# Two tiles' rows from early gathers, and three chunks of sines moved behind the setup block, in a fused embedding, attention and routing kernel

## The chip, the cores and the metric

The kernel runs on one core of a Trainium2 chip, as one launch. The metric is the device time of the launch in microseconds. The kernel before was timed three times: 1538.4, 1539.6 and 1539.77 us, median 1539.6 us.

## The reference

16384 tokens (128 sequences of 128) pass an embedding, one attention layer and one mixture layer. Cut to what matters here:

```python
# 1. token table: 12500 rows of 128 floats
freqs = arange(1, 129)
sin_table = sin((num_value / 1000)[:, None] * freqs[None, :])
table = where(is_num[:, None], sin_table, weight)
h = table[x]                                   # x: (128, 128) token numbers
# 2. attention with 8 heads of 64, per sequence of 128
n = (h - mean(h)) / sqrt(var(h) + eps)
q, k, v = n @ Wq, n @ Wkv
dots = where(eye, -1e-9, (q @ k.T) * scale)    # heads are mixed before ...
attn = mix_post(softmax(mix_pre(dots)))        # ... and behind the softmax
h = h + (attn @ v) @ Wout + bout
# 3. h + a shared feed-forward + two banks of 8 experts, top-1 routed, capacity 1280
```

All arithmetic is in float32. Matrix products that need the precision are built from three products of a high and a low part (`_hi`, `_lo`).

## The kernel before

Four blocks follow each other: setup, attention, experts, shared feed-forward. Each block holds one instruction list per engine (PE for matmuls, DVE for vector work, ACT for activations, POOL, and SP, which issues DMAs). The order within a list is written out by hand, and semaphores order the lists among each other. A block ends when all five lists have ended.

**Setup** builds the table in HBM. The 12500 rows are laid over 128 partitions, 97 rows each; the last 84 rows form a 98th column (`VS` = 98). Eight columns are a chunk (`VC` = 8), so there are 13 chunks (`CHUNKS`), and the last has two columns. SP loads the weight rows of each chunk into `h_sb`. The numbers of all rows are turned into thousandths by nine small DVE instructions (L553 to L561), split into halves (`num_hl`), transposed by PE, and copied to `numT` by ACT. Then chunk for chunk: PE multiplies numbers by frequencies (`angles`, into `ps_a`), ACT rounds to whole turns (`whole_turns`, L421), DVE subtracts them in two instructions (`reduce`, L584 and L585), POOL clamps (`clamp`, L340), ACT takes the sine (`sines`, L436), DVE puts the sines over the rows that are numbers (`put_sines`, L591, a predicated copy), and SP writes the chunk to the table (L401). Beside it the setup folds the attention weights into two matrices M and N: POOL and ACT make `mixed`, PE multiplies (`product`, L521), ACT and DVE split into `M_hi`, `M_lo`, `N_hi`, `N_lo`.

**Attention** handles one tile of 128 tokens at each step k, as a software pipeline over all engines that starts at k = -12 and is written as `step(i, k)` for each engine. POOL gathers the table rows of tile k+10 (L778, one indirect DMA each, into 8 buffers `got`), adds `bout` for tile k+7 (L785, five at once at k = -3), and computes deviations of four tiles at once (L806 to L808). DVE takes mean and variance of tile k+8 (L1112, L1121) and normalizes two tiles (L1039, `normalize`). PE transposes them (L874), ACT and DVE split them (L1000, L1139), PE multiplies with M into `ps_w` in four quarters q (L885 to L887), ACT and DVE split these (L992, L1081). Then come scores (L857), the predicated copy of the scores (L1066), the maximum (L1072), exponentials (L961), sums and products with N, the residual, and the router. In front of the pipeline PE runs `WARM` = 24 matmuls of the identity (L951).

Of the kernel before, what the change touches and what calls it, by code (L numbers as in the profile page):

```python
# [16 lines left out]
F32 = mybir.dt.float32  # L17
# [40 lines left out]
WARM = 24  # L58
# [10 lines left out]
VC = 8  # L69
CHUNKS = -(-VS // VC)  # L70

# [119 lines left out]

class RouterConstants:


    def __init__(self, sb):
# [8 lines left out]
        self.mv2 = [sb(f"mv2_{k}", [P, 4, 2]) for k in range(2)]  # L204
        self.token_i, self.token = sb("token_i", [P, TILES], I32), sb("token", [P, TILES])
# [32 lines left out]
def setup(nc, x, weight, num_value, is_num, Wq, Wkv, scale, mix_pre, mix_post, Wout,  # L238
# [6 lines left out]
    def rows_of(c):  # L245
        return VC if c < CHUNKS - 1 else VS - VC * (CHUNKS - 1)

    def cols(c):
        return slice(c * CH, c * CH + rows_of(c) * D)

    with ExitStack() as s:
# [10 lines left out]
        num_i = sb("num_i", [P, VS], I32)  # L262
        num_f = sb("num_f", [P, VS])
        part = sb("part", [P, 4, VS])
# [4 lines left out]
        mask = sb("mask", [P, VS], I32)  # L269
# [22 lines left out]
        names = ("made", "num", "num_f", "numT", "numT_out", "angle", "whole", "reduced", "clamped", "sine", "done", "put",  # L292
# [8 lines left out]
        LAST_COL = slice(VR * D, VS * D)  # L301

# [4 lines left out]
        def _(pool):  # L307
# [27 lines left out]
            made["head_of"] = link.n  # L335

            def clamp(c):
                a = angle[c % 3][:, 0:rows_of(c) * D]
                pool.wait_ge(S["reduced"], c + 1)
                nc.gpsimd.tensor_scalar(a, a, PI_BELOW, -PI_BELOW, ALU.min, ALU.max).then_inc(S["clamped"], 1)  # L340
# [6 lines left out]
            for c in range(CHUNKS):  # L347
# [20 lines left out]
                if c == 2:  # L368
                    link.wait()
                    link.inc(nc.gpsimd.tensor_copy(C.token[:, :], C.token_i[:, :]))  # L370
                    link.inc(nc.gpsimd.memset(zeros[:, :, D], float(DROPPED)))
            link.wait()

        @block.sync
        def _(sp):
            sp.dma_start(num_i[:, 0:VR], num_value[0:P * VR].rearrange("(p r) -> p r", p=P)).then_inc(S["num"], 16)
            sp.dma_start(isn[:, 0:VR], is_num[0:P * VR].rearrange("(p r) -> p r", p=P)).then_inc(S["num"], 16)
            sp.wait_ge(S["made"], made["pads"])
            sp.dma_start(num_i[0:REST, VR:VS], num_value[P * VR:VOCAB].rearrange("(p o) -> p o", o=1)).then_inc(S["num"], 16)
            sp.dma_start(rest_isn[0:REST, 0:1], is_num[P * VR:VOCAB].rearrange("(p o) -> p o", o=1)).then_inc(S["num"], 16)  # L380
# [6 lines left out]
            for c in range(1, CHUNKS - 1):  # L387
                need(sp, s_row[c % 4], 16 * (c // 4))
                sp.dma_start(h_sb[:, cols(c)], w_main[:, cols(c)]).then_inc(s_row[c % 4], 16)
            one = slice((CHUNKS - 1) * CH, VR * D)  # L390
            sp.wait_ge(s_row[(CHUNKS - 1) % 4], 16 * ((CHUNKS - 1) // 4))
            sp.dma_start(h_sb[:, one], w_main[:, one]).then_inc(s_row[(CHUNKS - 1) % 4], 16)
            sp.dma_start(h_sb[0:REST, LAST_COL], weight[P * VR:VOCAB, :]).then_inc(s_row[(CHUNKS - 1) % 4], 16)
# [5 lines left out]
            for c in range(CHUNKS - 1):  # L399
                sp.wait_ge(S["done"], c + 1)  # L400
                sp.dma_start(t_main[:, cols(c)], h_sb[:, cols(c)]).then_inc(S["put"], 16)  # L401
            sp.wait_ge(S["done"], CHUNKS)
            sp.dma_start(t_main[:, one], h_sb[:, one]).then_inc(S["put"], 16)
            sp.dma_start(table[P * VR:VOCAB, :], h_sb[0:REST, LAST_COL]).then_inc(S["put"], 16)
            sp.wait_ge(S["put"], 16 * (5 + CHUNKS + 1))

        @block.scalar
        def _(act):
# [3 lines left out]
            def rest_of_numbers():  # L412
                act.wait_ge(S["numT"], 2)
                nc.scalar.activation(numT[:, 4 * P:12 * P], ps_m[0:KR, :], ACT.Copy).then_inc(S["numT_out"], 1)
                nc.scalar.activation(numT[:, 12 * P:13 * P], ps_c[0:KR, 0:P], ACT.Copy).then_inc(S["numT_out"], 1)

            def whole_turns(c):
                w = rows_of(c) * D
# [14 lines left out]
            def sines(c):  # L433
                a = angle[c % 3][:, 0:rows_of(c) * D]
# [3 lines left out]
            for c in range(CHUNKS + 2):  # L438
# [18 lines left out]
                if c in (5, 6, 8):  # L457
                    remix({5: 1, 6: 2, 8: 3}[c])
                if c in (7, 9):
                    prefill((c - 7) // 2)  # L460
# [1175 lines left out]
```

## Time and profile before

| what | value |
| --- | --- |
| median of three runs | 1539.6 us |
| profiled execution | 1540.3 us |
| its span in the trace | 1538.6 us |
| busy: PE, ACT, DVE, POOL | 96%, 75%, 68%, 63% of the span |
| mean DMA rate | 82 GB/s |

Around the span lie 1.7 us that the trace doesn't show. The span can be cut by engine lists: setup until 67.7 us, where the first instructions of the attention block start, then the attention block. The slices of the page show PE at six to seven tenths busy in the first two slices of 38.5 us, nine tenths and more in nearly all that follow. The two first slices hold setup and the filling of the attention pipeline.

A row of the timeline says when a group of instructions started, how long they were busy together, the engine, the line, what is written from what, and in brackets how long the engine had been idle and what released it.

### The profile page before, as it was taken

The numbers are of one execution on the slowest core, as the hardware profiler recorded it, in microseconds if no ns is written. First come the engines' busy times: TensorE is split into PE (matmuls) and PEld (weight loads), VectorE is DVE, ScalarE is ACT, GpSimd is POOL, SyncE is SP. The second block draws the span as 40 slices with busy tenths as digits, with TensorE's granted clock in tenths as the row PEclk, the third lists the DMA queues.
The fourth block names the chain that finished last, engine by engine and source line by source line (L and its number), as shares of the span: only waits on it lengthen the run. The fifth ranks groups of instructions, "written<-read, shape, count | busy, mean of one in ns | idle before, by whom it ended". The sixth has DMA issues, their size and how long they took to land. (4 is left out here: it accounts for less than half of the span.)

```text
span 1538.6 us, 33795 instructions
## 1 busy us (share of the span) xinstructions
PE 1482.0 (96%) x11149; PEld 1371.7 (89%) x11149; DVE 1049.3 (68%) x2801; ACT 1146.6 (75%) x3461; POOL 971.1 (63%) x992
## 2 busy tenths in 40 slices
PE   6679999999999999999999999988999999999999
PEld 3368999999999999999999999978999999999999
DVE  7777787787877887787877887764334343346665
ACT  5468888888888888888888888874555555545555
POOL 6665558788788878878878887664577656510000
PEclk9889999999999999999999999999999999999999
DMA  6322321121121111111111111012344224456665
GB/s 254 137 105 105 115 66 52 52 67 40 40 59 38 39 57 35 35 49 42 34 35 54 35 35 51 25 39 62 80 114 114 72 69 109 119 152 186 184 182 149
DMA packets 170603, 126.35 MB, mean 82 GB/s; under 512 B 29539, under 2 KB 154061, under 8 KB 170432
## 3 DMA queue, kind: packets, MB, share of 16 engines
q1 hardware_dynamic: 153024, 104.05, 22.7%
q0 software_dynamic: 17408, 20.16, 4.8%
q8 instruction: 91, 1.49, 0.4%
q14 instruction: 80, 0.66, 0.2%
HBM read 61.63 MB, written 78.56 MB: 91 GB/s over the span
## 5 line engine op out<-in xcount | busy, mean ns | idle before, releaser
L961 ACT ACTIVATE expd<-masked,nmax 128x128 f32<-128x128 f32 x1024 | 395.7, 393 | 0.0
L763 POOL TENSOR_TENSOR prob<-expd,rtotal 128x1024 f32<-128x1024 f32 x128 | 243.0, 1898 | 143.4 <-DVE rtotal L1049 142.5
L1066 DVE COPY_PREDICATED masked<-off_diag,ps_s 128x1024 f32<-128x1024 int32 x128 | 175.2, 1369 | 146.9 <-PE ps_s L857 146.9
L899 PE MATMUL ps_o<-u,probT 128*128 128x128 f32 x2048 | 249.2, 275 | 2.9 <-issue 2.9
L899 PEld LDWEIGHTS ps_o<-u,probT 128*128 128x128 f32 x2048 | 239.1, 192 | 3.1 <-issue 3.1
L961 ACT ACTIVATION_READ_ACCUMULATOR expd<-masked,nmax 128x1 f32 x1024 | 196.5, 192 | 0.0
L970 ACT ACTIVATE u<-ps_ut 128x1024 f32<-128x1024 f32 x128 | 131.4, 1026 | 64.0 <-PE ps_ut L910 64.0
L1081 DVE TENSOR_TENSOR w_lo<-ps_w,w_hi 128x512 fp32r<-128x512 f32 x256 | 164.3, 680 | 4.3 <-ACT w_hi L992 4.3
L985 ACT ACTIVATE probT<-ps_ut 128x1024 f32<-128x1024 f32 x128 | 131.4, 1027 | 45.0 <-PE ps_ut L865 38.5
L992 ACT ACTIVATE w_hi<-ps_w 128x512 fp32r<-128x512 f32 x256 | 146.3, 596 | 18.6 <-PE ps_w L887 12.1
L885 PE MATMUL ps_w<-xT_hi,M_hi 128*128 128x256 f32 x512 | 155.2, 303 | 2.7 <-DVE xT_lo L1139 2.7
L1072 DVE TENSOR_REDUCE nmax<-masked 128x8 f32<-128x1024 f32 x128 | 155.5, 1215 | 2.5
L619 POOL DMA_INDIRECT sent_fq<-x,to_row x128 | 125.7, 982 | 42.0 <-issue 38.4
L619 POOL DMA_INDIRECT sent_sp<-x,to_row x128 | 130.9, 1022 | 31.3 <-issue 24.1
L778 POOL DMA_INDIRECT got<-table,gi x128 | 130.6, 1020 | 24.9 <-issue 12.6
L886 PE MATMUL ps_w<-xT_hi,M_lo 128*128 128x256 f32 x512 | 144.3, 282 | 0.0
L887 PE MATMUL ps_w<-xT_lo,M_hi 128*128 128x256 f32 x512 | 144.3, 282 | 0.0
L1564 ACT ACTIVATE sh_hid<-sh_ps_h,b 128x256 f32<-128x256 f32 x224 | 87.7, 475 | 75.4 <-PE sh_ps_h L1536 75.4
L865 PEld LDWEIGHTS ps_ut<-ident,prob 128*128 128x128 f32 x1024 | 115.3, 140 | 25.3 <-issue 15.5
L865 PE MATMUL ps_ut<-ident,prob 128*128 128x128 f32 x1024 | 133.6, 273 | 3.3 <-ACT u L970 3.3
L1427 POOL DMA_INDIRECT answers_fq<-res,tokens x80 | 81.1, 1014 | 54.5 <-DVE res L1406 37.5
L1545 PE MATMUL sh_ps_o<-w,sh_hid 128*128 128x128 f32 x896 | 109.1, 275 | 0.1
(231 smaller groups left out, 3881.4 us busy)
## 6 DMA issues: line engine op xcount, KB each, us to landing
turned<-x2T SPq DMA_DIRECT2D x32, 256.0 KB, 2.2
answers_sp<-zeros SPq DMA_DIRECT2D x16, 512.0 KB, 5.0
answers_fq<-zeros SPq DMA_DIRECT2D x16, 512.0 KB, 4.1
xT<-turned SPq DMA_DIRECT2D x56, 128.0 KB, 2.5
sh_back<-answers_sp SPq DMA_DIRECT2D x56, 128.0 KB, 2.3
sh_back<-answers_fq SPq DMA_DIRECT2D x56, 128.0 KB, 2.5
out<-res SPq DMA_DIRECT2D x56, 128.0 KB, 2.0
h_sb<-in_L_tok_weight SPq DMA_DIRECT2D x12, 512.0 KB, 5.7
```

The lines of the kernel that those rows point to most:

```text
L619: nc.gpsimd.indirect_dma_start(sent[b], bass.IndirectOffsetOnAxis(ap=to_row[(t // BATCH) % 2][:, c:c + 1], axis=0), x2[:, t % 16, :], None ...
L763: nc.gpsimd.tensor_tensor(prob[k % 2][:, :].rearrange("p (g j) -> p g j", g=H), expd[k % 2][:, :].rearrange("p (g j) -> p g j", g=H), rtot ...
L865: mm = nc.tensor.transpose(ps_ut[:, g * N:(g + 1) * N], prob[(k - 3) % 2][:, g * N:(g + 1) * N], ident[:, :])
L885: nc.tensor.matmul(o, M_hi, xT_hi[:, m % 4, :], start=True, stop=False)
L886: nc.tensor.matmul(o, M_lo, xT_hi[:, m % 4, :], start=False, stop=False)
L887: mm = nc.tensor.matmul(o, M_hi, xT_lo[:, m % 4, :], start=False, stop=True)
L899: mm = nc.tensor.matmul(ps_o[:, 0:D], probT[k % 2][:, g * N:(g + 1) * N], u[k % 2][:, g * D:(g + 1) * D], start=(g == 0), stop=(g == H - 1))
L961: ins = nc.scalar.activation(expd[(k - 1) % 2][:, g * N:(g + 1) * N], masked[(k - 1) % 2][:, g * N:(g + 1) * N], ACT.Exp, bias=nmax[(k - 1 ...
L992: nc.scalar.activation(w_hi[m % 2][:, :, 2 * q:2 * q + 2, :].rearrange("p b g j -> p g b j"), ps_w[q % 2][:, :].rearrange("p (g b j) -> p ...
L1066: nc.vector.copy_predicated(masked[k % 2][:, :].rearrange("p (g j) -> p g j", g=H), off_diag[:, :].unsqueeze(1).to_broadcast([P, H, N]), p ...
L1072: nc.vector.tensor_reduce(nmax[k % 2][:, :], masked[k % 2][:, :].rearrange("p (g j) -> p g j", g=H), X_AXIS, ALU.max, negate=True).then_in ...
L1081: nc.vector.tensor_tensor(dst, ps_w[q % 2][:, :].rearrange("p (g b j) -> p g b j", g=2, b=2), hi.bitcast(F32), ALU.subtract).then_inc(S["w ...
```

## The change

- SP loads the token numbers of the first two tiles (`ids0`) early. POOL gathers by them the numbers (`num_i`), the flags (`isn0`) and the weight rows of both tiles: six indirect DMAs in front of its first clamp. They become columns 99 and 100 of the layout in `h_sb` (`VX` = 100), so that the last chunk now has four columns. It is worked on as eighth of the thirteen (`ORDER`).
- The thousandths, the halves and the transpose of these columns are separate instructions (DVE after the second `reduce`, PE and ACT at the sixth chunk). Means and deviations of the two tiles are computed in the setup, and attention normalizes them from `h_sb`.
- The last three chunks in the new order (`LATES` = 3) are reduced and clamped in the setup, in unused columns of `h_sb`. Two of their sines run in the setup, the third first in attention's ACT list. Their predicated copies and their table writes stand at the start of the attention block, and POOL waits for these three writes (`s_late`) before its first gather, which is that of tile 2.
- DVE's list at the start of attention is written out anew: tile 0 and 1, late copies, four quarters of `w_lo`, then the statistics of tiles 2 and 3; those of tiles 4 to 7 and the normalization of tiles 2 and 3 stand inside step 0.
- `M_lo` moves behind the last `reduce`, and the identity matmuls (now 18) into the setup's PE list.

The diff, cut to its core:

```diff
-WARM = 24
+WARM = 18
+VX = VS + 2
+ORDER = (*range(7), CHUNKS - 1, *range(7, CHUNKS - 1))
+LATES = 3
+ON_TIME = CHUNKS - LATES
...
@@ setup, gpsimd
+            pool.wait_ge(S["ids0"], 16)
+            for t in range(2):
+                nc.gpsimd.indirect_dma_start(num_i[:, VS + t:VS + t + 1], None, num_value...).then_inc(S["num0"], 16)
+            for t in range(2):
+                nc.gpsimd.indirect_dma_start(isn0[:, t:t + 1], None, is_num...).then_inc(S["rows0"], 16)
+                nc.gpsimd.indirect_dma_start(h_sb[:, (VS + t) * D:(VS + t + 1) * D], None, weight, ...).then_inc(S["rows0"], 16)
...
+                if c == 10:
+                    link.wait()
+                    pool.wait_ge(S["stat0"], 1)
+                    link(nc.gpsimd.tensor_scalar(C.var[:, 0:2], C.mv1[0][:, 0:2, 1], 1.0, EPS, ALU.mult, ALU.add))
+                    link.inc(nc.gpsimd.tensor_tensor(C.rstd0[:, :], C.var[:, 0:2], C.power[:, 0:2], ALU.pow))
+            pool.wait_ge(S["clamped"], CHUNKS)
...
@@ setup, tensor
+                if c == 5:
+                    pe.wait_ge(S["num_f"], 2)
+                    pe.wait_ge(S["wT_out"], 3)
+                    number_rows(CHUNKS - 1).then_inc(S["numT"], 1)
                 if 5 <= c:
                     for half in range(2):
                         product((c - 5) // HC, (c - 5) % HC, half)
+            pe.wait_ge(S["reduced"], CHUNKS - 1)
+            for _ in range(WARM):
+                nc.tensor.matmul(ps_a[CHUNKS % 2][:, 0:P], ident[:, :], ident[:, :], start=True, stop=True)
...
@@ setup, vector
-            dve.wait_ge(S["num"], 64)
+            dve.wait_ge(S["num"], 32)
...
             for c in range(CHUNKS):
                 reduce(c)
-                if c >= 2:
+                if c == 1:
+                    dve.wait_ge(S["num0"], 32)
+                    thousandths(slice(VS, VX))
+                    halves(slice(CHUNKS - 1, CHUNKS), VX - VC * (CHUNKS - 1))
+                if 0 <= c - 2 < ON_TIME:
                     put_sines(c - 2)
...
-                if c == 11:
-                    dve.wait_ge(S["hi"], 1)
-                    link.inc(... mats["M_lo"] ...)
-            put_sines(CHUNKS - 2)
-            put_sines(CHUNKS - 1)
+                if c == 9:
+                    dve.wait_ge(S["done"], 8)
+                    for t in range(2):
+                        link.inc(nc.vector.bn_stats(C.stat0[:, t, :], h_sb[:, (VS + t) * D:(VS + t + 1) * D]))
+                    link.wait()
+                    for t in range(2):
+                        ins = nc.vector.bn_aggr(C.mv1[0][:, t, :], C.stat0[:, t, :])
+                    ins.then_inc(S["stat0"], 1)
+            dve.wait_ge(S["hi"], 1)
+            link.inc(... mats["M_lo"] ...)
...
@@ attention, sync
+            for n, c in enumerate(ORDER[ON_TIME:]):
+                sp.wait_ge(S["late_done"], n + 1)
+                sp.dma_start(t_main[:, chunk_cols(c)], h_sb[:, chunk_cols(c)]).then_inc(s_late, 16)
             load_expert(sp, bank, 0, first, first.loaded)
...
@@ attention, gpsimd
+                if k == -8:
+                    pool.wait_ge(s_late, 16 * LATES)
...
+                if k == -3:
+                    deviations(i, 0)
                 for t in range(5) if k == -3 else (k + 7,) if k > -3 and live(i, k + 7) else ():
...
@@ attention, vector
+                if k == 0:
+                    dve.wait_ge(S["first_rstd"], 1)
+                    normalize(2)
+                    low_x(1)
+                    first_stats(4, 4, S["stat1"])
...
+            normalize(0)
+            late_rows(0)
+            low_x(0)
+            late_rows(1)
+            dve.wait_ge(S["late_sine"], 1)
+            late_rows(2)
+            for q in range(4):
+                low_w(0, q)
+            first_stats(2, 2, S["first_stat"])
             pipelined(dve, step, BODY, FIRST, LAST, LEAD, END, link, VCHAIN)
```

How the instructions stand at three places, in the order of each engine's list.

DVE in the setup, from the second instruction of the second `reduce` on, before:

```order
L585 SCALAR_TENSOR_TENSOR angle<-turns,ps_a 128x1024
L584 SCALAR_TENSOR_TENSOR ps_a<-turns,ps_a 128x1024
L585 SCALAR_TENSOR_TENSOR angle<-turns,ps_a 128x1024
L591 COPY_PREDICATED h_sb<-mask,angle 128x1024
L584 SCALAR_TENSOR_TENSOR ps_a<-turns,ps_a 128x1024
```

and now, from the same instruction on (the third `reduce` follows behind these rows):

```order
L655 SCALAR_TENSOR_TENSOR angle<-turns,ps_a 128x1024
L621 CAST part<-num_i 128x2
L622 TENSOR_SCALAR part<-part 128x2
L623 TENSOR_SCALAR part<-part 128x2
L624 TENSOR_TENSOR part<-part 128x2
L625 TENSOR_TENSOR part<-part 128x2
L626 TENSOR_TENSOR part<-part 128x2
L627 SCALAR_TENSOR_TENSOR part<-part 128x2
L628 SCALAR_TENSOR_TENSOR part<-part 128x2
L629 SCALAR_TENSOR_TENSOR num_f<-part 128x2
L634 CAST num_hl<-num_f 128x4
L635 TENSOR_TENSOR num_hl<-num_f,num_hl 128x4
```

Eleven instructions on two columns have come between the second and the third `reduce`.

POOL at the start of attention, before. The rows start at the gathers of tiles 0 to 3 and end with that of tile 8:

```order
L778 DMA got<-table,gi 128x128 x4
L775 COPY gi<-ids 128x4
L778 DMA got<-table,gi 128x128
L792 TENSOR_SCALAR var<-mv_0 128x2
L793 TENSOR_TENSOR rstd<-var,power 128x2
L778 DMA got<-table,gi 128x128
L792 TENSOR_SCALAR var<-mv_0 128x2
L793 TENSOR_TENSOR rstd<-var,power 128x2
L778 DMA got<-table,gi 128x128 x2
L785 TENSOR_TENSOR h_sb<-got,bout_b 128x128 x5
L775 COPY gi<-ids 128x4
L778 DMA got<-table,gi 128x128
```

and now, from behind the gathers of tiles 2 and 3 to the gather of tile 8:

```order
L883 COPY gi<-ids 128x4
L887 DMA got<-table,gi 128x128 x2
L903 TENSOR_SCALAR var<-mv_0 128x2
L904 TENSOR_TENSOR rstd<-var,power 128x2
L887 DMA got<-table,gi 128x128 x2
L859 TENSOR_SCALAR var<-mv_1 128x4
L860 TENSOR_SCALAR var<-mv_0 128x4
L861 TENSOR_TENSOR rstd<-var,power 128x8
L896 TENSOR_TENSOR h_sb<-h_sb,bout_b 128x128 x2
L896 TENSOR_TENSOR h_sb<-got,bout_b 128x128 x3
L883 COPY gi<-ids 128x4
L887 DMA got<-table,gi 128x128
```

The deviations of tiles 4 to 7 (L859 to L861) have moved from behind the gather of tile 10 to in front of the gather of tile 8.

DVE in step 0 of attention, from the predicated copy of tile 0's scores to that of tile 1, before:

```order
L1066 COPY_PREDICATED masked<-off_diag,ps_s 128x1024
L1072 TENSOR_REDUCE nmax<-masked 128x8
L1081 TENSOR_TENSOR w_lo<-ps_w,w_hi 128x2x2x128 x2
L1039 TENSOR_SCALAR x_0<-got,mv_1,rstd 128x128 x2
L1112 BN_STATS stat<-got 128x6
L1121 BN_AGGR mv_0<-stat 128x2
L1066 COPY_PREDICATED masked<-off_diag,ps_s 128x1024
```

and now, from tile 3's statistics (in front of step 0) on. Behind this piece, three more pairs L1163 and L1165 follow, then the two `w_lo`, tiles 4 and 5 normalized, tile 8's statistics, and the copy for tile 1:

```order
L1163 BN_STATS stat<-got 128x6
L1165 BN_AGGR mv_0<-stat 128x2
L1194 COPY_PREDICATED masked<-off_diag,ps_s 128x1024
L1200 TENSOR_REDUCE nmax<-masked 128x8
L1140 TENSOR_SCALAR x_1<-got,mv_0,rstd 128x128 x2
L1147 TENSOR_TENSOR xT_lo<-ps_x,xT_hi 128x256
L1163 BN_STATS stat<-got 128x6
L1165 BN_AGGR mv_1<-stat 128x2
```

Between the first copy of scores and the second now stand ten instructions more: the normalization and the low part of tiles 2 and 3, and the statistics of tiles 4 to 7.

## Rows read from the trace of the kernel before

**Rows 1.** Windows: busy time of each engine in a stretch, clock, DMA share, GB/s.
```profile
116.00:1130.00 1014.00, 1002.48 (x7330) 919.08 (x7329) 763.42 (x2040) 849.59 (x2709) 751.46 (x752) 1.00 0.18 53
```
**Rows 2.** Waits of DVE, 13 to 66 us: total, times, longest.
```profile
DVE ps_a L584 <- ACT turns L421: 6.1, 4, 3.4
```
**Rows 3.** Timeline of the setup, DVE's chunk loop: start, busy, engine, line.
```profile
14.10 1.23 DVE L584 SCALAR_TENSOR_TENSOR ps_a<-turns,ps_a 128x1024 f32<-128x1024 int32 x1 [3.43 <-ACT turns L421]
...
51.20 1.30 DVE L591 COPY_PREDICATED h_sb<-mask,angle 128x1024 f32<-128x1024 int32 x1
52.40 1.23 DVE L584 SCALAR_TENSOR_TENSOR ps_a<-turns,ps_a 128x1024 f32<-128x1024 int32 x1
...
64.98 0.67 DVE L612 TENSOR_TENSOR N_lo<-ps_c,N_hi 128x512 fp32r<-128x512 f32 x1
```
**Rows 4.** Groups by line and shape, DVE, 4 to 13 us.
```profile
L554 DVE TENSOR_SCALAR part<-part 128x98 f32<-128x98 f32 x1 | 1.1, 1059 | 0.0
L553 DVE CAST part<-num_i 128x98 f32<-128x98 int32 x1 | 0.5, 457 | 4.5 <-DMA rest_isn<-in_L_tok_is_num 4.5
L566 DVE CAST num_hl<-num_f 128x2 fp32r<-128x2 f32 x1 | 0.2, 160 | 0.0
```
**Rows 5.** Timeline of the setup around the sixth and seventh chunk.
```profile
30.55 3.75 PE L521 MATMUL ps_m<-mixed,wkT 128*128 128x512 f32 x4 [0.79 <-POOL mixed L343]
30.72 0.59 ACT L454 ACTIVATE wvT<-ps_t 128x512 f32<-128x512 f32 x1
...
36.54 1.23 DVE L584 SCALAR_TENSOR_TENSOR ps_a<-turns,ps_a 128x1024 f32<-128x1024 int32 x1 [1.09 <-ACT turns L421]
```
**Rows 6.** Timeline around the end of the setup.
```profile
65.05 0.80 SPq L404 DMA_DIRECT2D table<-h_sb  x1
67.69 0.33 SPq L228 DMA_DIRECT2D w<-in_L_ffn_W_sp  x1
```
**Rows 7.** Waits of SP's queue, 60 to 68 us.
```profile
SPq L251 <- DMA table<-h_sb: 1.3, 1, 1.3
```
**Rows 8.** Timeline of SP from 59.7 us: three table writes, the first at 59.71.
```profile
59.71 4.79 SPq L401 DMA_DIRECT2D table<-h_sb  x3
```
**Rows 9.** Window of one microsecond behind that write.
```profile
62.00:63.00 1.00, 0.00 (x0) 0.00 (x0) 1.00 (x2) 0.00 (x0) 1.00 (x1) 0.50 0.00 0
```
**Rows 10.** DMA issues, 58 to 90 us: count, median us to landing.
```profile
got<-table,gi POOLq DMA_INDIRECT x11, 2.6
```
**Rows 11.** Timeline of POOL at the start of attention.
```profile
68.50 1.19 POOL L778 DMA_INDIRECT got<-table,gi  x1 [0.60 <-POOL gi L775]
...
71.27 0.95 POOL L778 DMA_INDIRECT got<-table,gi  x1 [0.30 <-issue]
...
80.94 2.11 POOL L785 TENSOR_TENSOR h_sb<-got,bout_b 128x128 f32<-128x128 f32 x5
...
83.45 0.99 POOL L778 DMA_INDIRECT got<-table,gi  x1 [0.27 <-POOL gi L775]
...
88.79 1.68 POOL L808 TENSOR_TENSOR rstd<-var,power 128x8 f32<-128x8 f32 x1
```
**Rows 12.** Timeline of DVE in attention's first steps.
```profile
72.40 0.29 DVE L1112 BATCH_NORM_STATS2 stat<-got 128x6 f32<-128x128 f32 x1 [6.74 <-DMA got<-table,gi]
...
88.32 1.37 DVE L1066 COPY_PREDICATED masked<-off_diag,ps_s 128x1024 f32<-128x1024 int32 x1 [1.02 <-PE ps_s L857]
...
92.99 1.33 DVE L1066 COPY_PREDICATED masked<-off_diag,ps_s 128x1024 f32<-128x1024 int32 x1
...
98.92 1.34 DVE L1066 COPY_PREDICATED masked<-off_diag,ps_s 128x1024 f32<-128x1024 int32 x1 [1.32 <-PE ps_s L857]
```
**Rows 13.** Timeline of PE: scores of tile 2 and of tile 4.
```profile
96.92 0.70 PE L857 MATMUL ps_s<-w_hi,xT_hi 128*128 128x512 f32 x2 [2.40 <-DVE w_lo L1081]
...
108.07 0.70 PE L857 MATMUL ps_s<-w_hi,xT_hi 128*128 128x512 f32 x2 [0.30 <-DVE w_lo L1081]
```
**Rows 14.** Window of two microseconds at tile 2's scores.
```profile
98.00:100.00 2.00, 2.00 (x10) 1.81 (x9) 1.08 (x1) 0.49 (x4) 1.73 (x3) 0.50 0.19 74
```

More of the change, by code:

```diff
@@ L301, in setup, with angle_of @@
         LAST_COL = slice(VR * D, VS * D)
+        loaded = {}
+        for i, c in enumerate(ORDER):
+            loaded[i] = loaded.get(i - 4, 0) + (32 if c == CHUNKS - 1 else 16)
+        def angle_of(i):
+            return angle[i % 3][:, 0:rows_of(ORDER[i]) * D] if i < ON_TIME else late_angles(h_sb, i - ON_TIME)
         made = {}
@@ L398, in _ @@
                 sp.dma_start(dst, src).then_inc(S["put"], 16)
[L399 to L405, printed above, removed]
+            for i, c in enumerate(ORDER[:ON_TIME]):
+                sp.wait_ge(S["done"], i + 1)
+                if c < CHUNKS - 1:
+                    sp.dma_start(t_main[:, cols(c)], h_sb[:, cols(c)]).then_inc(S["put"], 16)
+                else:
+                    sp.dma_start(t_main[:, one], h_sb[:, one]).then_inc(S["put"], 16)
+                    sp.dma_start(table[P * VR:VOCAB, :], h_sb[0:REST, LAST_COL]).then_inc(S["put"], 16)
+            for k in range(4):
+                sp.wait_ge(s_row[k], max(n for i, n in loaded.items() if i % 4 == k))
+            sp.wait_ge(S["put"], 16 * (5 + ON_TIME + 1))
         @block.scalar
@@ L530, in _ @@
             angles(1)
-            for c in range(4, CHUNKS):
+            for c in range(4, CHUNKS - 1):
                 ins = number_rows(c)
@@ L567, in _, with thousandths @@
-            link.wait()
-            for part_of, whole in ((slice(0, CHUNKS - 1), slice(0, VC)), (slice(CHUNKS - 1, CHUNKS), slice(0, last))):
-                n = VC if part_of.start == 0 else last
-                src = num_f[:, part_of.start * VC:part_of.start * VC + (part_of.stop - part_of.start) * n].rearrange("p (c r) -> p c r", r=n)
-                nc.vector.tensor_tensor(num_hl[:, part_of, whole, 1], src, num_hl[:, part_of, whole, 0].bitcast(F32),
-                                        ALU.subtract).then_inc(S["num_f"], 1)
+            def thousandths(at):
+                value, q, hi, lo = (part[:, n, at] for n in range(4))
+                link(nc.vector.tensor_copy(value, num_i[:, at]))
+                link(nc.vector.tensor_scalar(q, value, 0.001, None, ALU.mult))
+                link(nc.vector.tensor_scalar(hi, q, 4097.0, None, ALU.mult))
+                link(nc.vector.tensor_tensor(lo, hi, q, ALU.subtract))
+                link(nc.vector.tensor_tensor(hi, hi, lo, ALU.subtract))
+                link(nc.vector.tensor_tensor(lo, q, hi, ALU.subtract))
+                link(nc.vector.scalar_tensor_tensor(hi, hi, -1000.0, value, ALU.mult, ALU.add))
+                link(nc.vector.scalar_tensor_tensor(lo, lo, -1000.0, hi, ALU.mult, ALU.add))
+                link(nc.vector.scalar_tensor_tensor(num_f[:, at], lo, 0.001, q, ALU.mult, ALU.add))
@@ L689, in attention @@
         s_got = [sem(f"a_got{k}") for k in range(8)]
+        s_late = sem("a_late_put")
         s_sent = [sem(f"a_sent{k}") for k in range(8)]
@@ L948, in step @@
                         mm.then_inc(S["head_down"], 1)
-            for _ in range(WARM):
-                nc.tensor.matmul(ps_o[:, 0:D], ident[:, :], ident[:, :], start=True, stop=True)
             pipelined(pe, step, BODY, FIRST, LAST, LEAD, END)
```

243 lines of the change are left out of this document (141 added, 102 removed).

## The prediction

> **What bounds the kernel now.** I read the windows first. Behind 116 us PE is busy for 1002.5 of 1014 us at the full granted clock [rows 1], and nothing of the change touches what runs there. So the change counts only by how much earlier or later the attention pipeline reaches the state in which PE never waits. The scores of tile 4 are the marker for that: they start at 108.07 after a short wait for DVE [rows 13], and PE has nearly no gap behind them. The second view is the timeline from 0 to 108 us, followed backwards from there: tile 4's scores wait for `w_lo` from DVE, whose list from 88.32 on runs nearly without idle time [rows 12]. In front of it lies the chain table write, gather, statistics, deviation, normalize. The setup ends by a table write that SP waits 1.3 us for [rows 7]. DVE bounds the setup's chunk loop: all its waits there sum to 6.1 us, 3.4 of them ahead of the first `reduce` [rows 2, 3].
>
> **The setup, as DVE's sum.** Before, DVE runs from 14.10 to 65.65 [rows 3]. The terms, in us:
> - Start. DVE was released by the fourth of four small loads [rows 4] and now waits for the first two. SP issues them about 0.45 apart: -0.9.
> - Three full predicated copies leave. In the dense part one costs 52.40 - 51.20 = 1.2 [rows 3]: -3.6.
> - Eleven small instructions come behind the second `reduce`. Such a one is busy 0.16 [rows 4], 0.21 with the gap to the next dependent one: 2.3. From below 1.8. From above 4.5, because a like instruction took 1.06 [rows 4] while POOL worked, and here POOL clamps the second chunk meanwhile. I take 2.8, near the lower row, as only the first three have that form: +2.8.
> - The last chunk has four columns and not two: `reduce` +0.5, copy +0.3 (the 1024-wide 1.2 scaled by width): +0.8.
> - Flag copy, two statistics, two aggregations: 0.2 + 2 x 0.33 + 2 x 0.2: +1.3.
> - Waits. Before, beside the first, they are 6.1 - 3.4 = 2.7. The one ahead of the third `reduce` (1.4) is filled by the small instructions. The one ahead of the seventh (1.1) [rows 5] grows: PE now waits until ACT has copied `wvT`, done at 31.31, and transposes (0.4), while the products began at 30.55 [rows 5]. That puts the products, and the next chunk's angles behind them in PE's list, 1.2 later. Together about -0.4.
>
> The sum is 0.0: DVE ends at about 65.65 again. What the copies free, the added work takes. But the block then ends by DVE and no longer by the write: before, the wait ended at 65.85 + 1.3 = 67.15 and the next block began at 67.69 [rows 6, 7], so the change of blocks costs 0.55. Now it begins at 66.2: **-1.5**. POOL's last clamp ends about half a microsecond before DVE. The six gathers cost POOL 1.25 each [rows 11] in a stretch in which its list was empty, from about 8.5 until the first `reduce` ends at 14.10 + 2 x 1.23 = 16.6 [rows 3]: 7.5 in 8.1, hidden, with no room to spare. The identity matmuls now lie beside the last `reduce`. That costs nothing.
>
> The Trainium skill, page "GPSIMD Engine Reference", in the table of the engine's properties, has GpSimd share its SBUF interfaces with VectorE, with contention where a VectorE instruction uses both ports. By it the first three small instructions could each wait for the clamp, and the small ones would cost 4.5, not 2.8. The 1.06 row [rows 4] agrees with it, but does not show it alone.
>
> **Attention, counted from the start T of its block.** Before, T = 67.69. Tile 8's gather starts at T+15.8 [rows 11] and the copy of tile 1's scores at T+25.3 [rows 12].
>
> Now DVE first normalizes (0.65), makes three late copies (3 x 1.2) and a low part (0.4): T+4.65. Only then can the third late write be issued. A write of this size issued at 59.71 had left the queues by 62.0 [rows 8, 9]; with completion I take 2.5 (bounds 2.3 and 3.4). POOL's first gather starts at T+7.15 and the second 1.25 later, landing 2.6 behind its start [rows 10]: T+11.0. The upper bound for a landing is 72.40 - 68.50 = 3.9 [rows 11, 12]. Tile 0's scores are ready at about T+10.3 (by the early rows this is 9 us sooner than before), but DVE's statistics of tiles 2 and 3 stand ahead of their copy, so that begins at T+11.6.
>
> Then DVE's list: copy 1.35 [rows 12], maximum 1.2 (the same width), normalize 0.6, the round over PE and ACT for the low part 1.4, four pairs of statistics 2.4 (an estimate, 0.6 a pair): T+18.6. POOL waits for these: deviations 1.7 [rows 11] and two small instructions ahead, 2.25 together; five additions 2.1 [rows 11]; index copy with its gap 0.5; and only then tile 8's gather, at T+23.5 where it was T+15.8. It lands 2.6 later. DVE's statistics of tile 8 stand in front of the copy of tile 1's scores: T+26.7 with the pair's 0.55. Against T+25.3 that is **+1.4**. So the nine microseconds won on tile 0's scores are all given back at the gather of tile 8.
>
> From there the list is as before. Before, the next copy is 5.93 later and waits 1.32 for tile 2's scores [rows 12], which took 2.0 because the clock went to 0.50 in their last third (granted 0.50 from 98 to 100 [rows 14]). With six equal passes, four at 2.4 and two at 1.2 GHz, all six cost 1.5 at 2.4 GHz and 3.0 at 1.2 GHz. PE now idles some 7 us ahead of these scores where it was 2.4 [rows 13], so I expect them at 1.2 GHz for the most part: between -0.5 and +1.0, **+0.9** taken. ACT is further ahead: **-0.3**, a small wait of DVE for it at tile 3.
>
> **Sum.** -1.5 + 1.4 + 0.9 - 0.3 = +0.5. The profiled execution took 1540.3 us (span 1538.6 and 1.7 around it) and would take 1540.8. It lies 0.7 above the median of the runs, so the forecast is 1540.1 us. About 3.1 us (0.2%) is what a measurement of this kernel can tell from no change.
>
> The terms' bounds: setup from 2.5 earlier to 2.5 later than my value (small instructions 1.8 to 4.5, the wait at the seventh chunk 0 to 2.3), write and gathers from -0.5 to +2.2, clock from -1.4 to +0.1. The likeliest case alone covers 1537 to 1543.
>
> **Rivals.**
> 1. *The gather of tile 8 is not what DVE waits for* (faster). If POOL is through sooner, or the gathers land sooner, the copy of tile 1's scores follows tiles 4 and 5's normalization: deviations end at T+20.9, normalize 0.6 and a pair 0.55, so T+22.1, 4.6 less. That gives 1535.5, and 1534.8 with tile 2's scores half at the full clock. For it: the whole early part is ready nine microseconds sooner. Against it: the order of POOL's list, which is fixed, and 1.25 a gather. Chance 0.24.
> 2. *PE's clock* (slower). PE has only scattered work from T+10 to T+31. If it stays at 1.2 GHz not for tile 2's scores only but until tile 4's, two more scores (+1.5 each by the estimate above) come onto the path, which gives 1543.1, and more if it falls again later. It decides from the point at which PE, and not DVE, ends last at tiles 3 and 4. For it: 0.50 at 98 us after a gap of only 2.4 us. Against it: DVE has 5 us of work per tile, which covers a slow PE in part. Chance 0.14. The Trainium skill, page "TensorE: Matmul & The Clock Gate", section "HAM oscillation — how this bites in real kernels", tells of kernels whose PE falls to half rate in every wait and starts each piece cold. By that rule this rival is the case, and the trace agrees at 98 us.
> 3. *The rebuilt setup is longer* (no measurable change, or slower). Six gathers hold the first clamp, the small instructions cost 4.5, PE's wait at the sixth chunk passes on in full: DVE ends 2.5 later, 1542.6. For it: none of these has room to spare. Chance 0.12.
>
> The forecast keeps 0.50. Faster by more than 0.2%: nearly all of rival 1 and 0.02 of the forecast's own spread, 0.25. Slower: 0.11 of rival 2, 0.05 of rival 3, 0.04 of the forecast, 0.20. The rest is 0.55. Range 1535.0 to 1543.4.
>
> **What would show it.** Right: DVE's last instruction of the setup within a microsecond of 65.6 and the attention block from about 66.2; eleven small instructions in 2 to 3.5 us; POOL's first gather 7 us into the block and that of tile 8 near T+23.5, with DVE's longest wait named after it; tile 4's scores within 1.5 us of 108.1. Wrong: no wait of DVE for that gather, a block start outside 64 to 68.5, PE at half pace for tiles 3 and 4, or any difference behind 116 us, where I expect none.

## The result: 0.14% slower, and the profile after

The changed kernel takes 1540.05 us (median of 20 runs, 1537.91 to 1543.35), the kernel before 1538.04 us in as many runs beside it (1536.56 to 1540.22). The ratio is 1.0014, interval [1.0007, 1.0020]: 2.0 us slower, inside the 0.2% that the prediction counted as no change, and 0.05 us from its 1540.1. That close a hit is luck, since two errors cancel. The forecast was a change of +0.5, and the two profiled spans differ by 2.2 (1538.6 and 1540.8): 1.7 more. But it was added to 1539.6, the median of the first three runs of before, and twenty runs have 1538.04: 1.6 less.

Where the 2.2 us arise is seen in three places. First the setup, in the timeline of DVE after (start, busy, engine, line, operation, in brackets the idle time before it and what ended it):

```profile
13.38 1.23 DVE L654 SCALAR_TENSOR_TENSOR ps_a<-turns,ps_a 128x1024 f32<-128x1024 int32 x1 [1.08 <-ACT turns L480]
...
18.18 0.16 DVE L621 CAST part<-num_i 128x2 f32<-128x2 int32 x1
18.37 1.04 DVE L622 TENSOR_SCALAR part<-part 128x2 f32<-128x2 f32 x1
19.44 0.31 DVE L623 TENSOR_SCALAR part<-part 128x2 f32<-128x2 f32 x1
19.79 0.16 DVE L624 TENSOR_TENSOR part<-part 128x2 f32<-128x2 f32 x1
...
21.25 1.22 DVE L654 SCALAR_TENSOR_TENSOR ps_a<-turns,ps_a 128x1024 f32<-128x1024 int32 x1
...
38.46 1.23 DVE L654 SCALAR_TENSOR_TENSOR ps_a<-turns,ps_a 128x1024 f32<-128x1024 int32 x1 [2.16 <-ACT turns L480]
...
52.14 1.60 DVE L212 COPY_PREDICATED h_sb<-is_number,angle 128x512 f32<-128x512 int32 x1
...
65.75 0.68 DVE L692 TENSOR_TENSOR N_lo<-ps_c,N_hi 128x512 fp32r<-128x512 f32 x1
67.04 0.60 DVE L1140 TENSOR_SCALAR x<-h_sb,mv,first_rstd 128x128 f32<-128x128 f32 x2 [0.61 <-PEq L278]
```

The first `reduce` is 0.72 sooner than in [rows 3], the eleven small instructions take 3.1 us (18.18 to 21.25), one of them 1.04 for two columns, the copy of the four-column chunk takes 1.60, and the seventh `reduce` is 1.9 later than in [rows 5] behind a wait of 2.16 instead of 1.09. DVE ends at 66.43. The block starts at T = 67.02 instead of 67.69, 0.67 sooner.

Second POOL, from the block's start on, the rows that answer to [rows 11]:

```profile
67.02 0.18 POOL L883 COPY gi<-ids 128x4 int32<-128x4 int32 x1 [1.79 <-POOLq L278]
75.48 1.10 POOL L887 DMA_INDIRECT got<-table,gi  x1 [8.28 <-DMA table<-h_sb]
...
86.77 0.19 POOL L859 TENSOR_SCALAR var<-mv 128x4 f32<-128x4 f32 x1 [2.68 <-DVE mv L1165]
87.04 0.19 POOL L860 TENSOR_SCALAR var<-mv 128x4 f32<-128x4 f32 x1
87.32 1.66 POOL L861 TENSOR_TENSOR rstd<-var,power 128x8 f32<-128x8 f32 x1
88.97 0.87 POOL L896 TENSOR_TENSOR h_sb<-h_sb,bout_b 128x128 f32<-128x128 f32 x2
89.80 1.29 POOL L896 TENSOR_TENSOR h_sb<-got,bout_b 128x128 f32<-128x128 f32 x3
91.05 0.18 POOL L883 COPY gi<-ids 128x4 int32<-128x4 int32 x1
91.51 1.08 POOL L887 DMA_INDIRECT got<-table,gi  x1 [0.28 <-POOL gi L883]
```

The first gather waits 8.28 us for the third late write, and tile 8's, the last row, has deviations and additions ahead of it: T+24.5 where it was T+15.8. What DVE makes of that (answering to [rows 12]):

```profile
71.53 0.69 DVE L1153 TENSOR_TENSOR w_lo<-ps_w,w_hi 128x512 fp32r<-128x512 f32 x1
...
78.34 0.29 DVE L1163 BATCH_NORM_STATS2 stat<-got 128x6 f32<-128x128 f32 x1 [2.45 <-DMA got<-table,gi]
...
79.98 1.26 DVE L1194 COPY_PREDICATED masked<-off_diag,ps_s 128x1024 f32<-128x1024 int32 x1
...
94.17 0.29 DVE L1241 BATCH_NORM_STATS2 stat<-got 128x6 f32<-128x128 f32 x1 [4.25 <-DMA got<-table,gi]
94.50 0.18 DVE L1250 BATCH_NORM_AGGREGATE mv<-stat 128x2 f32<-128x6 f32 x1
94.60 1.27 DVE L1194 COPY_PREDICATED masked<-off_diag,ps_s 128x1024 f32<-128x1024 int32 x1
...
101.41 1.34 DVE L1194 COPY_PREDICATED masked<-off_diag,ps_s 128x1024 f32<-128x1024 int32 x1 [2.25 <-PE ps_s L956]
```

Tile 0's copy begins at 79.98, tile 1's only at 94.60, behind a wait of 4.25 us for tile 8's gather. That is T+27.6, where before it was T+25.3. Third the clock, in PE's timeline (answering to [rows 13]) and in windows (busy time of each engine, then the granted clock, DMA share, GB/s; answering to [rows 14] and [rows 1]):

```profile
98.47 1.19 PE L956 MATMUL ps_s<-w_hi,xT_hi 128*128 128x512 f32 x2 [6.69 <-DVE w_lo L1153]
99.46 1.05 PE L956 MATMUL ps_s<-w_lo,xT_hi 128*128 128x512 f32 x2
100.31 1.05 PE L956 MATMUL ps_s<-w_hi,xT_lo 128*128 128x512 f32 x2
...
110.27 0.70 PE L956 MATMUL ps_s<-w_hi,xT_hi 128*128 128x512 f32 x2 [0.32 <-DVE w_lo L1153]
```

```profile
116.00:1130.00 1014.00, 1002.26 (x7315) 918.30 (x7315) 763.40 (x2039) 849.42 (x2713) 751.84 (x751) 1.00 0.18 52
...
98.00:100.00 2.00, 1.53 (x4) 1.27 (x5) 1.13 (x5) 0.43 (x3) 0.76 (x1) 0.50 0.15 41
100.00:102.00 2.00, 2.00 (x8) 1.71 (x7) 0.59 (x1) 0.00 (x0) 1.73 (x3) 0.50 0.00 0
```

PE has idled 6.69 us and makes all of tile 2's scores at the half clock (granted 0.50, 1.2 GHz), so tile 2's copy stands 6.81 behind tile 1's instead of 5.93: +0.88. Tile 4's scores come 8.86 behind that copy instead of 9.15: -0.29. The sum is -0.67 + 2.28 + 0.88 - 0.29 = 2.2, the marker's own shift (110.27 against 108.07) and the whole difference of the spans. Behind 116 us PE is as busy as before.

### The profile page after: what moved, and what is told of

Read it like the earlier page. It is cut to its first block and busy times, and to the rows that moved or that the text cites. A ratio compares the mean times of both kernels' runs of the same rounds, so it can differ in the third digit from the quotient of the medians.

```text
span 1540.8 us, 33791 instructions
## 1 busy us (share of the span) xinstructions
PE 1483.2 (96%) x11137; PEld 1370.2 (89%) x11137; DVE 1055.4 (68%) x2811; ACT 1147.2 (74%) x3461; POOL 974.1 (63%) x996
## 5 line engine op out<-in xcount | busy, mean ns | idle before, releaser
L699 POOL DMA_INDIRECT sent_sp<-x,to_row x128 | 131.0, 1024 | 32.8 <-issue 24.5
```

The costliest lines, as they stand in the source:

```text
L699: nc.gpsimd.indirect_dma_start(sent[b], bass.IndirectOffsetOnAxis(ap=to_row[(t // BATCH) % 2][:, c:c + 1], axis=0), x2[:, t % 16, :], None ...
```

## The experiments

Twelve runs, each timed twelve times, on three chips: e1 to e4 on one, c0 and e5 to e7 on the second, e8 to e11 on the third. The kernel before, beside them, takes 1570.6 to 1573.0 us there. The traces of such runs show more idle time on PE behind 800 us, not in the part studied here. Each ratio is against the kernel before on the same chip, with an interval some 0.3% wide, so the trace has to decide most questions. All times below are of this table: T is the start of POOL's first instruction in the block; "copy 1" is the start of tile 1's copy; "2 - 1" what tile 2's copy comes behind it; "scores 4" the start of tile 4's scores.

| run | 7th reduce (its wait) | T | first gather | copy 1 | 2 - 1 | scores 4 | ratio, interval |
|---|---|---|---|---|---|---|---|
| c0_after | 37.52 (1.21) | 66.29 | T+8.48 | 93.57 | 6.82 | 109.55 | 1.0026 [1.0010, 1.0041] |
| e1_gather8_first | 37.75 (1.46) | 66.32 | T+8.55 | 89.74 | 6.86 | 105.27 | 0.9981 [0.9965, 0.9996] |
| e2_loads_behind_writes | 37.94 (1.65) | 66.53 | T+8.14 | 94.67 | 6.81 | 110.64 | 1.0036 [1.0017, 1.0054] |
| e3_filler | 37.52 (1.22) | 66.76 | T+8.45 | 96.23 | 6.94 | 111.84 | 1.0019 [1.0004, 1.0033] |
| e4_transpose_later | 37.40 (1.09) | 65.96 | T+8.46 | 93.56 | 6.80 | 109.11 | 1.0011 [0.9994, 1.0028] |
| e5_no_small_ones | 35.57 (0.98) | 64.36 | T+8.44 | 91.70 | 6.81 | 107.69 | 1.0025 [1.0009, 1.0041] |
| e6_gather8_and_transpose | 36.86 (0.57) | 65.44 | T+8.57 | 88.86 | 6.73 | 104.25 | 0.9992 [0.9975, 1.0008] |
| e7_filler26 | 38.45 (2.16) | 67.03 | T+8.40 | 95.79 | 5.56 | 110.03 | 1.0015 [0.9995, 1.0035] |
| e8_best_and_filler16 | 37.25 (0.95) | 65.83 | T+8.54 | 89.23 | 6.52 | 104.42 | 0.9982 [0.9967, 0.9998] |
| e9_two_late | 38.44 (2.16) | 68.53 | T+7.25 | 94.78 | 6.81 | 110.25 | 1.0006 [0.9991, 1.0020] |
| e10_two_late_and_best | 37.38 (1.08) | 67.47 | T+7.28 | 89.61 | 6.46 | 104.76 | 0.9963 [0.9943, 0.9982] |
| e11_warm24 | 38.45 (2.17) | 67.13 | T+8.50 | 95.82 | 6.81 | 111.80 | 1.0020 [1.0009, 1.0032] |

**The changed kernel again.** Its edit is none.

> The changed kernel itself, once more, beside the kernels below on one chip. First measurement: 1.0014 [1.0007, 1.0020] times before. Expected: the same within 0.1%, tile 4's scores about 43 us after the attention block's first instruction (110.27 - 67.02 there).

The ratio is 1.0026, 0.12% above the first 1.0014, with an interval that holds it. T+43.3 for tile 4's scores, as expected. The seventh `reduce`, though, comes at 37.52 and not at 38.46, with nothing changed. The timeline of PE of this run shows why:

```profile
32.49 3.28 PE L584 MATMUL ps_m<-mixed,wkT 128*128 128x512 f32 x4
35.70 0.72 PE L549 MATMUL ps_a<-freq,numT 16*128 16x512 f32 x2
```

and that of the changed kernel's first trace:

```profile
32.47 3.75 PE L584 MATMUL ps_m<-mixed,wkT 128*128 128x512 f32 x4
36.15 1.22 PE L549 MATMUL ps_a<-freq,numT 16*128 16x512 f32 x2
```

The same products start at the same time. Two passes of the angles behind them take 0.72 us in one execution and 1.22 in the other, where PE's passes get this short only from 41 us on. The windows give a granted clock of 1.00 for both stretches, so here the durations have to tell the clock: two passes of this width take 0.70 at tile 4's scores, at the full clock, and 1.19 at tile 2's, at the half clock. That is worth 0.9 us at this `reduce` and varies between executions, so single traces of the setup are compared below only where these products have the same duration.

**Tile 8's and 9's gathers first.**

```diff
 # POOL, step k == -3
+fetch(-2)          # gathers of tiles 8 and 9, taken out of the next two steps,
                    # without their wait for `resid`
+fetch(-1)
 deviations(i, 0)
 # then the five additions
```

> The changed kernel, but POOL issues the gathers of tiles 8 and 9 right behind that of tile 7, ahead of the deviations of tiles 4 to 7 and the five additions (their buffers are free, since tiles 0 and 1 no longer use them). Theory A (DVE's wait for the gather of tile 8, 4.25 us, gives back what the early tiles win): that wait is gone, the copy of tile 1's scores starts at about T+23.7 instead of T+27.6 (T the start of the attention block), the scores of tile 4 start some 3.8 us earlier, near 106.5, and the time falls by 3 to 4 us against the changed kernel, 1 to 2 us below the kernel before. Rival B (PE's clock sets the pace of the first steps): the wait goes, but the scores of tile 4 move by less than 1.5 us. Rival C (the rebuilt setup is the loss): no more than 1 us.

POOL's and DVE's timelines of this run:

```profile
83.94 0.97 POOL L889 DMA_INDIRECT got<-table,gi  x1 [0.27 <-POOL gi L884]
85.22 0.95 POOL L889 DMA_INDIRECT got<-table,gi  x1 [0.31 <-issue]
```

```profile
89.32 0.28 DVE L1247 BATCH_NORM_STATS2 stat<-got 128x6 f32<-128x128 f32 x1
89.74 1.33 DVE L1200 COPY_PREDICATED masked<-off_diag,ps_s 128x1024 f32<-128x1024 int32 x1
```

The wait of 4.25 us in front of tile 8's statistics is gone, tile 1's copy stands at T+23.4 instead of T+27.3 (c0), tile 4's scores 4.3 sooner than in c0 (5.0 sooner than in the first trace, where 3.8 was expected; 0.7 of it lies in the start of the block), and the kernel is faster than before. The gather of tile 8, held by POOL's own list, is what cost the time: theory A.

**The weight loads behind the late writes.**

```diff
+sp.wait_ge(s_late, 16 * LATES)
 load_expert(sp, bank, 0, first, first.loaded)
```

> The changed kernel, but SP waits for the three late table writes before it issues the first expert's weight loads. Theory A (the third write lands 3.9 us behind its issue because it shares the queues with the other late writes and with these loads): POOL's first gather starts 1.0 to 1.3 us earlier in the block (T+7.3 and not T+8.5), and so does everything up to the scores of tile 4; the time falls by about 1 us. Rival (a write of this size takes that long by itself, or the pile-up is among the three writes): the first gather moves by less than 0.4 us and the time stays.

The first gather comes at T+8.14, 0.34 sooner than in c0: so little of the late landing is due to the loads. The loads now run beside the gather instead, and its reader waits longer: the statistics of tile 2 start 4.3 behind its gather's start, 3.1 in c0 (one execution each). The rival is right, and nothing is gained.

**Identity products ahead of tile 2's scores, 40 and 26.**

```diff
 # PE, behind step 1's liftings (range(26) in e7)
+for _ in range(40):
+    nc.tensor.matmul(ps_o[:, 0:D], ident[:, :], ident[:, :], start=True, stop=True)
```

> The changed kernel, and 40 identity matmuls on PE in step 1, in the 6.7 us in which PE now waits for tile 2's w_lo. Theory A (the idle time in front of tile 2's scores lets the clock fall, and these six passes at 1.2 GHz cost 2.9 us instead of 1.5): the granted clock stays at 1.00 from 92 to 102 us, tile 2's scores end 0.9 to 1.4 us earlier, and DVE's wait for them falls from 2.25 to about 1; the time falls by about 1 us. Rival (DVE's work hides the slow clock): the scores of tile 4 move by less than 0.3 us.

> The changed kernel with 26 instead of 40 identity products of 128 columns on PE ahead of tile 2's scores; 40 had run past the point where the scores could start (101.49 instead of near 100.1). Theory A (the half clock costs 0.9 us in tile 2's scores and has no later effect): scores at full clock, tile 2's copy 5.9 to 6.1 us behind tile 1's (6.81 in the changed kernel), tile 4's scores 0.8 us sooner; time 0.05% under, which the timing hardly shows. Rival B (the clock is at full speed again through tile 2's own scores anyway; the filler only moves where it rises): copy 6.8 behind, nothing gained.

The timelines of PE, first of the 40 and then of the 26:

```profile
92.64 9.09 PE L991 MATMUL ps_o<-ident 128*128 128x128 f32 x80
101.49 0.71 PE L956 MATMUL ps_s<-w_hi,xT_hi 128*128 128x512 f32 x2
```

```profile
99.69 0.70 PE L956 MATMUL ps_s<-w_hi,xT_hi 128*128 128x512 f32 x2 [1.89 <-DVE w_lo L1156]
100.23 0.62 PE L956 MATMUL ps_s<-w_lo,xT_hi 128*128 128x512 f32 x2
100.69 0.62 PE L956 MATMUL ps_s<-w_hi,xT_lo 128*128 128x512 f32 x2
```

I had priced an identity product at 0.1 us. It is two passes and takes 0.22, so 40 of them took 8.9 us (92.64 to 101.49) and held up the scores that they were to speed up: the expectation for e3 failed by that. With 26 the scores run at full clock and tile 2's copy is 5.56 behind tile 1's instead of 6.81. From tile 1's copy to tile 4's scores it is 14.24 instead of 15.98 (c0) or 15.67 (the first trace). So the half clock costs 1.25 there, the gain holds up to tile 4, and a clock that falls in a wait is a real cost here: what the Trainium skill tells on the page "TensorE: Matmul & The Clock Gate", section "HAM oscillation — how this bites in real kernels", holds in this place, for 1.25 us and for one tile's scores. Against c0 the marker did not improve all the same, since DVE waits longer for tile 8's gather: 5.24 us here and 4.91 in e3, where the seven runs without filler and with that gather in its old place have 4.20 to 4.27. The wait grows behind the gather's start: from it to the statistics pass 3.7 us in e7 and 3.3 in e3, 2.7 in the first trace. The DMA view of e7 from 93 to 94 us, while the gather is under way, has one transfer of another queue, which it calls `q8 instruction`; e3 has one in the same microsecond; in the seven others it comes behind 96 us, when the gather has landed. That the products on PE pull this transfer forward, onto the gather, fits both runs, but is not shown.

**The last chunk's transpose a chunk later.**

```diff
-if c == 5:        # PE, and ACT's copy likewise
+if c == 6:
     pe.wait_ge(S["num_f"], 2)
```

> The changed kernel, but the transpose of the last chunk's numbers, with its wait for ACT's copy of wvT, stands one chunk later in PE's list (behind the angles of the seventh chunk), and ACT's copy of it ahead of that chunk's remix. Theory A (this wait delays PE's products and the angles behind them, so that DVE waits 2.2 us and not 1.1 for the seventh reduce, and the delay runs through to the end of the setup): DVE's wait falls to about 1.1, DVE's last setup instruction and the scores of tile 4 come about 1 us earlier, the time falls by about 1 us. Rival (the next wait takes its place, as the eighth chunk's angles now need the transposed numbers soon after): less than 0.3 us.

The products of the mixing matrices start at 31.40 instead of 32.49, and the seventh `reduce` waits 1.09 instead of 2.16. Against the first trace, whose products also ran at the half clock, the block starts 1.06 sooner and tile 4's scores are 1.16 sooner. The pair e9 and e10 shows it a second time at like clock (38.44 and 37.38). Theory A; the timing alone could not tell it.

**The eleven small instructions left out.**

```diff
+halves(slice(CHUNKS - 1, CHUNKS), 2)     # ahead, with the first splitting
 # DVE, behind the second reduce
-dve.wait_ge(S["num0"], 32)
-thousandths(slice(VS, VX))
-halves(slice(CHUNKS - 1, CHUNKS), VX - VC * (CHUNKS - 1))
```

> The changed kernel without the eleven instructions that make the pairs of the two gathered columns (3.1 us between the second and the third reduce on DVE, 18.18 to 21.33); the thousandths of the gathered numbers are left out of the computation, and a small cast pair stands in the first splitting. Theory A (they stand on the path of the sines): the third reduce starts near 18.3 instead of 21.3, and the attention block's start moves from 67.0 to 64.2 (by up to 3 us, less 0.2 for the larger splitting); tile 1's copy and tile 4's scores move along by as much: time 0.18% under the changed kernel's. Rival B (the setup is bound by PE's products of the mixing matrices or by the sine engine, which fill the gap): the block starts less than 1 us sooner.

```profile
19.31 1.23 DVE L655 SCALAR_TENSOR_TENSOR ps_a<-turns,ps_a 128x1024 f32<-128x1024 int32 x1 [1.05 <-ACT turns L480]
```

This kernel leaves the thousandths of the first two tiles' numbers out of the computation. The third `reduce` starts 1.96 sooner than in c0 and not 3, because it now waits 1.05 for ACT: a third of the small work had lain in a wait. T and tile 4's scores both move by 1.9. The setup passes this on in full: theory A, smaller by the wait. The ratio (1.0025) does not show the 1.9 us.

**Both gains together, and with 16 identity products.** e6 is e1 and e4 in one; e8 adds the loop of e7 with 16.

> Both edits that brought something in the first four together: tile 8's and 9's gathers right behind tile 7's, and the last chunk's transpose a chunk later. If they add (theory A: one acts on the setup's end, the other on the gathers behind it), tile 4's scores start 5.0 + 1.1 = 6.1 us before the changed kernel's 110.27, near 104.2, less 0.7 that the first may have had by chance; time 0.34% under the changed kernel's, ratio to before about 0.998. Rival: the later start of the gathers' wait (the third write) eats the transposes' share, since the write's landing is bound by the amount of data: then only 5.0.

> The version with tile 8's and 9's gathers behind tile 7's and the late transpose, and 16 identity products on PE in the gap ahead of tile 2's scores (2.42 us of PE's idle time there, which 16 products of 0.1 us at the half clock fill but for 0.7). Theory A (what PE did ahead sets the clock of tile 2's scores, as 26 of them did in the changed kernel, where tile 2's copy came 5.56 us behind tile 1's instead of 6.81): tile 2's copy 5.6 to 6.0 us behind tile 1's (6.73 without them), tile 4's scores 0.7 to 1.0 us sooner, near 103.4; ratio to before near 0.998. Rival B (16 are too few: the clock stays at its half through these scores): 6.7 behind and nothing gained, or up to 0.3 lost.

In e6 tile 4's scores are at 104.25, 5.3 before c0's and 6.0 before the first trace's (expected 6.1). They add. In e8 the 16 products take 3.7 us (twice what I had priced), so that the scores start at 94.08 at full clock, with no gap ahead: the copies are 6.52 apart instead of 6.73. They start 4.9 behind tile 1's copy, 0.9 more than in e6 (3.9), which eats the clock's gain. As e10 has 6.46 without any filler, even the 0.2 are not shown. Neither theory was tested as meant, since 16 were too many and not too few.

**Two late chunks, alone and with both gains.**

```diff
-LATES = 3
+LATES = 2          # and one `late_rows` less in DVE's list at the start of attention
```

e10 has the edits of e6 besides.

> The changed kernel with two chunks' sines taken beside attention's first turns instead of three. Theory A (the first gather waits for the last late write, which waits for three writes' data, 1.5 MB at 300 to 400 GB/s): the third write's share, 1.3 us of DVE and up to 1.4 us of pile-up, moves ahead of the block; one copy (1.3 us) goes back into the setup, so the block starts 1.2 to 1.4 us later, and the first gather comes 6.0 to 6.9 us behind it instead of 8.48: tile 4's scores from 0.4 later to 0.8 sooner than 109.55. Rival B (the last write lands as long after its issue with two as with three): first gather 7.2 behind, tile 4's scores at the same time within 0.2.

> Two late chunks, with tile 8's and 9's gathers behind tile 7's and the late transpose. If the effects add: 104.25 plus what two late chunks alone bring or cost against 109.55 (-0.8 to +0.4), ratio to before 0.998 to 0.9995. Rival: with the gathers no longer in the way, DVE's own work is the bound up to tile 1's copy, and the copy moved into the setup costs its 1.3 us in full: near 105.5.

e9 against the first trace (seventh `reduce` at 38.44 and 38.46): T is 1.5 later, the first gather 1.2 nearer to T, tile 1's copy 0.2 later, tile 4's scores at 110.25 and 110.27. Rival B: the last write lands as long after its issue with two as with three, and one copy more or less in the block is an even exchange. The view of the late writes' line (`--source L811`) gives their times from issue to landing, the longest being the last write's:

```profile
DMA to landing us min/median/max: 2.6/2.6/3.1
```

for the changed kernel,

```profile
DMA to landing us min/median/max: 2.6/2.8/3.0
```

for e9, and for e2, without the loads beside them:

```profile
DMA to landing us min/median/max: 2.6/2.6/2.7
```

e10 has tile 4's scores at 104.76, 0.1 above the upper end of what was expected (103.45 to 104.65) and below the rival's 105.5, and the lowest ratio of all, 0.9963 [0.9943, 0.9982]: a version that beats both kernels, the one before by 0.2 to 0.6%. That it beats e1, e6 or e8 is not shown; their intervals overlap, and its marker is no earlier than theirs.

**24 products at the setup's end instead of 18.**

```diff
-WARM = 18
+WARM = 24
```

> The changed kernel with 24 identity products at the end of the setup, as before, instead of 18. Theory A (PE waits for the first lifting of the block anyway, and the clock falls in the wait for the gathers whatever stands ahead of it): nothing: tile 1's copy 27.3 us behind the block's start, tile 4's scores 43.3 behind, ratio as the changed kernel's (1.0014 to 1.0026). Rival B (six products less let the clock fall sooner, and this is a part of the 2 us lost): the first tile's matrices at full clock, tile 0's scores up to 1.5 us sooner, ratio near 1.0005.

T = 67.13 and scores of tile 2 at the half clock, as with 18. But the first tile's matrices (`ps_w`) ran at the full clock here. Their passes take 0.28 us, but for two of 0.36 and 0.39, where the first trace, with 18, has rows like this one:

```profile
70.23 0.41 PE L986 MATMUL ps_w<-xT_hi,M_lo 128*128 128x256 f32 x1
```

The granted clock from 70 to 72 us is 0.50 in the first trace and 1.00 in e11, and all twelve traces with 18 products have a part of these matrices at the half clock. Tile 0's scores start at T+8.4, earlier than in any of those (T+8.7 to T+9.6). So the half of rival B that speaks of the clock came true. It is worth nothing, because DVE reaches the copy of these scores only behind the statistics of tiles 2 and 3, whose gathers have yet to land. Tile 3's gather landed later in this run (a wait of 1.53 ahead of its statistics instead of 0.70), which puts tile 4's scores at T+44.7, 1.4 more than c0. There is no gain at the marker from more products: theory A's result, and rival B's gain is out.

**All together.** The four versions with tile 8's gather moved have tile 4's scores at 104.7 on average and a mean ratio of 0.9980; the other eight 110.1 and 1.0020. That is 5.4 us in the marker and 0.40%, 6.3 us, in the time: on average, what is won or lost at tile 4 stays to the end.

## Why the prediction was right, and which terms were off

- **Where the change counts.** Right: no difference behind 116 us, the marker's shift is the span's. The marker itself is outside what the prediction named as its sign of being right: tile 4's scores at 110.27, and not within 1.5 of 108.1. The first gather, 8.5 into the block and not 7, is off as well; the block's start, the small instructions, tile 8's gather and DVE's longest wait are as it said, within about a microsecond.
- **Setup, forecast -1.5, measured -0.7.** This is one of the two steps that failed, in size: DVE ends 0.8 later than the sum has it. The start came 0.7 and not 0.9 sooner; the small instructions took 3.1 and not 2.8, one of them 1.04 beside POOL's clamp, as the upper bound had it for three (by its rows that bound is 5.0: 2.3 and three times 0.9); those two are 0.5 of the 0.8. DVE's waits behind the first were 2.2 against 2.3 in the sum, so the 1.1 by which PE's late transpose delays the seventh `reduce` (e4) was priced rightly. The rest is 0.4, and two of the terms for the added work explain it to within 0.1. The copy of the last chunk, priced at +0.3 by its width, takes 1.60 for 512 columns where before it took 0.42 for 256: some 0.9 too little. Flag copy, statistics and aggregations took 0.9 and not 1.3. The change of blocks costs 0.6, as forecast.
- **The gathers' chain, forecast +1.4, measured +2.3.** The other step that failed, in size. Right in kind, wait for wait: e1 shows that tile 8's gather behind POOL's deviations and additions is the cause, and that rival 1 is what one gets when it is moved. Too small was the way from the third write's issue, T+4.6 as forecast, to the first gather: 3.9 instead of 2.5. Of the 1.4, 0.6 are the landing itself: 3.1 behind the issue instead of 2.5, and 2.7 in e2, so 0.4 of them go with the weight loads. The other 0.8 pass between that landing and POOL's start, which no term of the sum held. e2 shows them a second way: SP, which waits there for the same three writes, issues its first load at 73.92, POOL its gather at 74.67. From the first gather on the forecast ran 0.4 long (T+7.15 to T+26.7, 19.55, against 19.1). The Trainium skill, page "DMA: Bandwidth & Descriptors", section "Anatomy of one DMA — SWDGE (gpsimd) path", has a fixed 2.0 us and the bytes at 436 GB/s for DMAs that GpSimd issues, an estimate of 3.2 for these 512 KB. The late writes, which SP issues, landed after 2.6 to 3.1, nearest to it when the loads run beside the write.
- **Clock, forecast +0.9 and -0.3, measured +0.88 and -0.29.** Right, and e7 confirms what is behind the first. Behind the second is DVE's wait for ACT ahead of tile 3's copy, 0.30 before and now gone, as forecast. Rival 2 in its full form (half pace up to tile 4) did not come.
- **Rivals.** 1 did not happen, but e1 produces it: tile 1's copy 3.9 us sooner, forecast 4.6, and the marker 4.3. 3 did not happen: POOL's six gathers end at 16.06 and the first clamp starts at 16.10, so that they had just room. DVE ended 0.8 later than forecast and not 2.5.

## What to carry to other kernels

When a dependency at the front of a pipeline is relieved, follow the list of the engine that issues the next transfers: work won on the first tile is given back where that list, in its fixed order, comes to the transfer that the second tile needs. Issue transfers ahead of arithmetic on the same engine wherever both are ready. Price a DMA that another DMA depends on to the start of the dependent instruction, not to the landing. Take the time that a forecast change is added to from as many runs as the result will have: here it was 1.6 us off by itself, and 2.0 us were to be told.

## What was not expected of the hardware

- The third write's landing to the first gather's start on POOL took about 0.8 us (e2: issued at 71.2, landed after 2.7, gather at 74.67).
- A `tensor_scalar` on two columns took 1.04 us beside POOL's clamp (18.37 and 18.35, both 1.04 long); its like a microsecond later took 0.31, others 0.16. The copy of 512 columns that took 1.60 starts at 52.14, 0.03 behind a clamp of 1.04 as well. The Trainium skill's page "GPSIMD Engine Reference", cited in the prediction, names such a contention in its section "Specifications"; that the small instruction ends together with the clamp agrees with it.
- By the durations of its passes, PE's clock rose within the products of 32 to 36 us in one execution and at 41 us in another of the same kernel, 0.9 us in a setup of 67. The granted clock of the windows reads 1.00 in both.
